# Attention 2 in 32-row quadrants, value products in 32 columns, and projections with the gate biases in their chunks

## The reference

```python
h = tok(x)                                   # layernorm, 768 -> 192, layernorm, class token: 197 x 192
# attention 1
q, k, v = split(layernorm(h) @ w_qkv.T)      # 12 heads of 64
q = q * rsqrt(norm(q over the heads) + 1e-8) # k likewise
h = h + softmax(q @ k.T / scale[head]) @ v @ w_out.T + b_out
# attention 2
x2 = layernorm(h)
probs = softmax(x2 @ Wg.T + bg); combine = the two largest of 8, the rest 0
hw = (x2 @ A + ba) * combine                 # 8 experts, rank 16: 128 columns
qkv = x2 @ Wqkv.T + bqkv + 2 * (hw @ Bm + combine @ bb)
q, k, v = split(qkv)                         # 12 heads of 16
h = h + softmax(q @ k.T / 4) @ v @ Wproj.T + bproj
```

## Time and profile before

| | |
|---|---|
| median of 3 runs | 4209.02 us (4180.69 to 4213.12) |
| the profiled execution | 4172.1 us, span 4170.0 us |
| TensorE busy | 3646.2 us, 87% |
| VectorE busy | 2701.7 us, 65% |
| ScalarE busy | 2236.3 us, 54% |
| GpSimd busy | 523.2 us, 13% |
| mean granted TensorE clock | 0.974 |

### The profile page before, as it was taken

How to read it: one execution, slowest core, us unless ns; L and a number is a source line. 1 busy time by engine, 2 the same in 40 slices (tenths; PEclk the granted TensorE clock), 3 DMA queues, 4 the chain that set the end, 5 groups by cost and what they waited for, 6 DMA issues and landing times.

```text
span 4170.0 us, 92080 instructions
## 1 busy us (share of the span) xinstructions
PE 3646.2 (87%) x37528; PEld 3010.9 (72%) x37528; DVE 2701.7 (65%) x6870; ACT 2236.3 (54%) x4033; POOL 523.2 (13%) x858
## 2 busy tenths in 40 slices
PE   3888988988988988889889889889889889898887
PEld 2777777777777777777777777777777777777776
DVE  4566666666676676676666666666766766766654
ACT  1555555555555555555555555555555555555553
POOL 1111101111101101111111111111011011011110
PEclk8999999999999999999999999999999999999997
DMA  3000000000000000000000000000000000000000
GB/s 84 9 9 16 16 9 16 16 9 16 16 9 16 16 9 16 16 9 16 9 15 16 9 16 16 9 16 16 9 16 16 9 16 16 9 16 16 9 4 4
DMA packets 26635, 60.62 MB, mean 15 GB/s; under 512 B 3626, under 2 KB 16557, under 8 KB 26222
## 3 DMA queue, kind: packets, MB, share of 16 engines
q1 hardware_dynamic: 26222, 54.73, 4.3%
HBM read 45.04 MB, written 9.68 MB: 13 GB/s over the span
## 4 chain that ended last, share of the span: by engine, by line
PE 59%; DVE 34%; ACT 3%; issue 2%; POOL 1%; DMA 0%; SPq 0%; DVEq 0%; ACTq 0%
PE psum L604 13%; DVE mx L952 13%; PE psum L638 6%; PE psum L610 6%; PE psum L577 6%; PE psum L668 3%; PE psum L543 3%; PE psum L533 3%; DVE kb L1047 3%; PE psum L661 3%; PE psum L640 2%; DVE qk_sq L925 2%; DVE qk L940 2%; PE psum L641 2%; PE psum L620 2%
## 5 line engine op out<-in xcount | busy, mean ns | idle before, releaser
L952 DVE TENSOR_REDUCE mx<-psum 99x4 f32<-99x788 f32 x768 | 703.6, 969 | 17.4 <-PE psum L561 10.4
L757 ACT ACTIVATE ebuf<-psum 99x788 f32<-99x788 f32 x768 | 604.9, 824 | 172.8 <-PE psum L593 160.6
L449 POOL TENSOR_TENSOR veps<-mv,eps_ln 99x2 f32<-99x2 f32 x256 | 49.7, 194 | 3005.9 <-DVE mv L861 2407.9
L638 PE MATMUL psum<-hn_s,qkv_w 96*128 96x197 f16 x2304 | 342.2, 254 | 44.2 <-ACT ss L730 43.0
L533 PE MATMUL psum<-hn_s,qk_w 128*128 128x197 f16 x3840 | 363.4, 250 | 1.2 <-DVE hn_s L918 1.2
L973 DVE TENSOR_TENSOR qk<-psum,rinv 128x197 f32<-128x197 f32 x384 | 137.5, 358 | 342.2 <-ACT rinv L766 342.2
L717 ACT ACTIVATE qk_sq<-psum 128x788 f32<-128x788 f32 x192 | 158.8, 827 | 352.5 <-PE psum L533 352.5
L533 PEld LDWEIGHTS psum<-hn_s,qk_w 128*128 128x128 f16 x3840 | 335.3, 98 | 7.5 <-DVE hn_s L918 1.5
L604 PE MATMUL psum<-ebuf,vx 98*64 98x197 f32 (+1 forms) x3072 | 332.7, 337 | 0.0
L591 PE MATMUL psum<-qa,ka 128*99 128x197 f16 x1536 | 289.2, 252 | 43.7 <-DVE qb L964 28.2
L604 PE MATMUL psum<-ebuf,ones_col 98*64 98x197 f32 (+1 forms) x3072 | 323.3, 330 | 0.0
(11 more groups left out here) (171 smaller groups left out, 7963.4 us busy)
## 6 DMA issues: line engine op xcount, KB each, us to landing
xb<-x_t SPq DMA_DIRECT2D x64, 591.0 KB, 3.7
out<-h SPq DMA_DIRECT2D x128, 73.5 KB
out<-h SPq DMA_DIRECT2D x64, 0.8 KB
vx<-w_qk SPq DMA_DIRECT2D x2, 384.0 KB
qk<-w_qkv SPq DMA_DIRECT2D x1, 720.0 KB
qk_sq<-w_emb SPq DMA_DIRECT2D x1, 576.0 KB
out_w<-w_out SPq DMA_DIRECT2D x1, 576.0 KB
vx<-w_qk SPq DMA_DIRECT2D x1, 576.0 KB
```

Source lines behind the costliest of these rows:

```text
L638: nc.tensor.matmul(o, qkv2_w[:, w, c, f], hn2_s[s][:, v, c, 0:NT], start=(c + w + v == 0), stop=False)
L757: nc.scalar.activation(ebuf[n % EBUFS][:].rearrange("p e a t -> p e (a t)"), psum[0:TR, b:b + 2, 0:2 * NT], ACT.Exp).then_inc(done, 1)
L952: nc.vector.tensor_reduce(mx[s][:, :, 2 * i:2 * i + 2].rearrange("p a e -> p e a"), psum[0:TR, b:b + 2, 0:2 * NT].rearrange("p e (a t) -> ...
```

## The change

**Attention 2 in quadrants.** Each head of 16 gets rows 32j to 32j+31 of the array. Three column blocks become two (`QKV2` from 960 to 704 columns). Two of the three groups of four heads share a block, and for them the keys are scaled with a mask that keeps one of two 16-row halves (`kmask`); the third has its own block. SM2 has three parts instead of six, each of 8 matmuls of 32 rows in four banks; ST2 has three parts of 32 matmuls in four banks: high x high, high x low, low x high and the negated maximum (`sel2`, `neg_t2`) for four heads. The eight masked copies are gone. The first two banks of SM2 and ST2 are released on their own (`rd_lo`). NT2 has one copy on ScalarE and none on VectorE.

**Value products in 32 columns.** PV has three parts of four heads instead of six of two: sums first, in a bank of their own, then the values in two halves of 32 columns. ScalarE starts on the sums (`sums_made`) before the values are done, and one multiplication of 394 columns replaces two of 197.

**Projections.** The hidden vector stands in a chunk of 128 rows and one of 64, which is there twice, once high and once low (`BIASED`). The last rows of the second take the gates (27 rows), so the bias product goes. A block takes eight matmuls. T2 makes 128 rows a chunk, and ScalarE doubles 64 columns of the layernorm's result first (`hn2_doubled`).

**Order and loads.** `ORDER` is new; one line of the old and one of the new stand in the diff. The weights need 49 load instructions on SyncE instead of 24, since they are placed piece by piece.

```diff
 ORDER = """
...
-N.2 -V2@2 -SM2.0@4 -SM2.1@2 N.3 -SM2.2@0 V.0@4 -SM2.3@2 -SM2.4@0 -SM2.5@6 V.1@4 SM.0@0 -NT2@7
+N.2 -V2@2 -SM2.0@4 -SM2.1@0 N.3 V.0@4 -SM2.2@0 V.1@6 SM.0@4 -NT2@0 SM.1@6 SM.2@2 -ST2.0@4 SM.3@0
...
-WIDE = ("QK", "V", "SM", "ST", "QK2", "SM2", "ST2")
+WIDE = ("QK", "V", "SM", "ST", "PV")
+QUAD = ("SM2", "ST2")
...
+            BIASED = ((0, 0, 0), (0, 1, 0), (1, 0, 0), (2, 0, 1), (3, 1, 1))
...
                     elif kind == "SM2":
-                        wait(pe, now, rd_sig["QK2"], ("QK2", s, 1))
-                        wait(pe, now, ka2_ready, ("QK2", s, 1))
-                        for e in range(2):
-                            h = 2 * i + e
-                            for t in range(2):
-                                mm = nc.tensor.matmul(ps(p, slice(0, TR), slice(NT * t, NT * t + NT), e),
-                                                      qa[s][:, h // 4, tile_cols(t)],
-                                                      ka[s][:, h, 0:NT], start=True, stop=True)
+                        wait(pe, now, high_QK2, ("QK2", s, 1))
+                        for t in range(2):
+                            for j in range(4):
+                                r = slice(32 * j, 32 * j + 32)
+                                mm = nc.tensor.matmul(ps(p, slice(0, TR), slice(NT * t, NT * t + NT), j),
+                                                      qh2[r, i // 2, tile_cols(t)], kh2[r, i, 0:NT],
+                                                      start=True, stop=True)
...
                     elif kind == "ST2":
+                        wait(pe, now, rd_sig["QK2"], ("QK2", s, 1))
                         wait(pe, now, rd_sig["NT2"], ("NT2", s, 0))
...
+                        for t in range(2):
+                            terms = ((kh2[:, i, tile_cols(t)], qh2[:, i // 2, 0:NT]),
+                                     (kh2[:, i, tile_cols(t)], ql2[:, i // 2, 0:NT]),
+                                     (kl2[:, i, tile_cols(t)], qh2[:, i // 2, 0:NT]),
+                                     (sel2[:, i, :], neg_t2[s][:, 0:NT]))
+                            for n, (left, right) in enumerate(terms):
+                                for j in range(4):
+                                    r = slice(32 * j, 32 * j + 32)
+                                    mm = nc.tensor.matmul(ps(p, slice(0, TR), slice(NT * t, NT * t + NT), j),
+                                                          left[r], right[r], start=(n == 0), stop=(n == 3))
                     elif kind == "PV":
-                        wait(pe, now, rd_sig["ST"], ("ST", s, i))
+                        wait(pe, now, rd_sig["ST"], ("ST", s, 2 * i + 1))
...
-                        for at in (0, NT):
+                        for c in (2, 0, 1):
                             for t in range(2):
                                 n = key_rows(t)
...
+                                    mm = nc.tensor.matmul(
+                                        ps(p, slice(32 * j, 32 * j + 32), slice(NT * (c % 2), NT * (c % 2) + NT), c // 2),
+                                        left, eb[0:n, j % 2, t, :], start=(t == 0), stop=(t == 1))
+                            if c == 2:
+                                mm.then_inc(sums_made[1], 1)
...
                     elif kind == "QK2":
                         wait(pe, now, rd_sig["T3"], ("T3", s, 0))
...
+                        for m in range(2):
+                            o = ps(p, slice(0, 128), slice(NT * m, NT * m + NT))
+                            f = slice(128 * (2 * i + m), 128 * (2 * i + m) + 128)
+                            for n, (w, v, c) in enumerate(BIASED):
+                                nc.tensor.matmul(o, qkv2_w[:, w, f], hn2_s[s][:, v, c, 0:NT],
+                                                 start=(n == 0), stop=False)
+                            for n, (w, v) in enumerate(SPLIT):
+                                mm = nc.tensor.matmul(o, lorab_w[:, w, f], hw_s[s][:, v, 0:NT],
+                                                      start=False, stop=(n == 2))
...
-                        if i == 1:
-
-                            wait(act, now, high_QK2, p)
-                            for j in range(4):
-                                a = nc.scalar.mul(ka[s][:].rearrange("p (g j) t -> p g j t", j=4)[:, :, j, :],
-                                                  high2[:], masks[:, j:j + 1])
-                            a.then_inc(ka2_ready[1], 1)
...
+                            for u in range(2):
+                                nc.scalar.mul(kh2[:, u, 0:NT], psum[:, b, 0:NT], kmask[:, u:u + 1])
+                            nc.scalar.mul(kh2[:, 2, 0:NT], psum[:, b, NT:2 * NT], 1 / WS).then_inc(high_QK2[1], 1)
...
-                            for j in range(4):
-                                a = nc.vector.tensor_scalar(
-                                    kb[s][0:64].rearrange("p (g j) t -> p g j t", j=4)[:, :, j, :], low2[:],
-                                    masks[0:64, j:j + 1], None, ALU.mult)
+                            for u in range(G2):
+                                a = nc.vector.scalar_tensor_tensor(
+                                    out=kl2[:, u, 0:NT], in0=pair[:, u // 2],
+                                    scalar=kmask[:, u:u + 1] if u < 2 else 1 / WS,
+                                    in1=kh2[:, u, 0:NT], op0=ALU.mult, op1=ALU.subtract)
```

## The result

The changed kernel takes 4264.33 us (median of four runs, 4261.64 to 4265.76) beside 4209.94 of the kernel before on the same chip: a ratio of 1.0133, 95% interval 1.0084 to 1.0182. It is slower by 1.3%, where I forecast 4155 us and a gain.

What follows compares the result with a forecast made beforehand. No engine alone sets the time: VectorE ends stage A and limits stage B, TensorE mainly stage C. Terms -2.5 + 3.4 - 2.1 and 0.4 for the clock make -0.8 us a half pass, -55 in all: 4155 us, range 4040 to 4300.

Steps and rivals of the forecast that it cites:

- stage A: From output projection OP to SM2.0's first maximum on VectorE, 30.4 us: gains 2.5 us a half pass (bounds 1.9 and 2.9).
- stage B: From SM2.0's first maximum to attention 1's negated maxima, 12.8 us: loses 3.4 us a half pass (bounds 1.4 and 4.8).
- stage C: From attention 1's negated maxima to the next OP, 19.8 us, mainly TensorE: gains 2.1 us (bounds 1.2 and 3.0).
- these 4.7 us: TensorE work saved in stage A: 3.8 us in QK2 and some 0.9 in V2, mostly hidden because VectorE ends the stage.
- the walk: Row-by-row timing of stage C: ST.0 at +1.1 us, PV.2 at +13.1, next OP at +17.7, a gain of 2.1.
- rival of two pairs: Groups of four in ST2 take 0.17 instead of 0.085 us: 1.4 us more in stage B, 4241 us; chance 0.10.
- The 0.9 us ahead of PV.2: Stage C: PV.2 stands right behind ST.5 and waits 0.9 to 1.0 us for its exponential on ScalarE.
- M2.0's place in VectorE's way: Stage B: PV2.0 and M2.0 ahead of SM.5 put negated maxima at 16.2 instead of 12.8 us; VectorE idles before M2.0.
- rival of a shorter chain: Chain to M2.0 in stage B is shorter, 2 of the 3.4 us don't show: 4028 us; chance 0.16.
- TensorE bounds everything: TensorE's ten microseconds of saved work a half pass come off whole: ratio 0.85, 3580 us; chance 0.05.
- The clock: TensorE nearly idle from V2's end to V.0: one fall to half clock every half pass, 0.4 us over today's mean.
- The clock stays down: Falls also land on thin TensorE stretches from V.1 to ST.0: 2.2 us a half pass over the sum, 4292 us; chance 0.27.

Runs made afterwards that it cites:

- run 9: Kernel before with the change's projections alone, plus extra unread matmuls ahead of T2, QK2.0 and SM2.0: 4106.82 us, ratio 0.9802.
- run 7: Changed kernel with its waits filled by extra matmuls, but the old value products of attention 1 (six parts of two heads): 4130.20 us.
- run 4: Changed kernel with SM.5 ahead of PV2.0 and NT right behind it, waits filled by extra matmuls: 3991.21 us, ratio 0.9559.
- run 2: Changed kernel with extra unread matmuls only in the waits of stage B and stage C, 80 a half pass: 4175.59 us, ratio 1.000.
- run 1: Changed kernel with 206 extra unread matmuls a half pass in TensorE's waits: 4082.73 us, 0.9778 of the kernel before.
- run 10: Changed kernel with extra unread matmuls only in stage A's waits, 126 a half pass: 4266.70 us, ratio 1.0185.
- run 11: Changed kernel, unfilled, reordered: SM.5 ahead of ST2.1, NT and ST.0 ahead of ST2.2, ST.4 and ST.5 ahead of PV.1: 4049.99 us, ratio 0.9667.
- run 13: Changed kernel, waits unfilled, with ten extra matmuls (0.49 us) on the path at the end of OP: 4263.43 us.
- run 14: Changed kernel with its waits filled by extra matmuls, plus ten more on the path at the end of OP: 4116.71 us.

## Why the prediction was wrong

**At full clock it was right, step by step.** The filled kernels, with the fall of the clock taken out of both sides, give each step apart (us a half pass):

| | forecast | measured, filled |
|---|---|---|
| stage A | -2.5 | 30.37 to 27.90, -2.5 |
| stage B | +3.4 | 12.82 to 16.09, +3.3 |
| stage C | -2.1 | 19.84 to 17.90, -1.9 |
| sum | -1.2 | 63.03 to 61.90, -1.1 |
| of it the projections (run 9) | | -0.7 |
| of it the value products (run 7) | | -0.8 |
| of it the rest, by subtraction: quadrants and order | | +0.4 |

"Little of these 4.7 us reaches the end, because VectorE ends the stage" holds: in the changed kernel QK2 takes 0.69 us a block (forecast 0.68), and the first maximum starts 6.87 us after N.0 (forecast 6.9). In stage C the terms of the forecast don't add up to its gain: 3.7 us of work less, against 2.4 to 2.5 us of new waits, leave 1.2 to 1.3. The 2.1 comes from the walk, and the measured 1.9 bears out the walk. A group of four takes 0.09 us. Timeline of the changed kernel, TensorE, the first and the last of ST2.0's eight groups:

```profile
2041.80 0.29 PE L615 MATMUL psum<-qh,kh 32*99 32x197 f16 x4 [0.95 <-DVE mx L1004]
...
2042.41 0.28 PE L615 MATMUL psum<-neg_t,sel 32*99 32x197 f16 x4
```

Seven steps in 0.61 us, 0.087 each, so the rival of two pairs is out. There my estimate from the Trainium skill (TensorE: Matmul & The Clock Gate, Part 3: Packing small matmuls), 0.11 us, was too high; the trace decides. The 0.9 us ahead of PV.2 are 0.97. M2.0's place in VectorE's way is real: run 4 takes 2.4 us from B by it, so the rival of a shorter chain is out too. "TensorE bounds everything" is far off. The first OP starts at 123.97 instead of 122.21, 2 us later (forecast 5), but in other runs with the same loads it starts between 122.34 and 124.38, so the start's cost isn't clear of its scatter. The end gives 8 us (forecast 10).

**The step that failed is the one headed "The clock":** "I expect a fall in every half pass, 0.4 us over today's mean." It is 2.95 falls, and they cost 64.85 - 61.90 = 2.95 us; the kernel before loses 63.21 - 63.03 = 0.2 in the profiled execution. The forecast looked for the falls in one place, ahead of V.0, and there it was about right: the short fall at 29.6 us costs nothing, the long one at 26 us 0.5 us (and 1.15 in run 2, where it comes at 28). It put three other places at nothing. The trace of the changed kernel has 62 half passes, and their stages price the falls against the filled kernel (us):

| | half passes | A | B | C |
|---|---|---|---|---|
| filled, no fall (run 1) | | 27.90 | 16.09 | 17.90 |
| falls at 26 (long), 40 and 47 us | 37 | 27.90 | 17.71 | 19.33 |
| falls at 9, 30 and 47 us | 22 | 29.23 | 16.10 | 19.36 |

So a fall after T2 (9 us) costs 1.3 us, the one from ST2.1 to PV2.0 (40 us) 1.1 of the 1.6 in B, and the one from ST.0 to PV2.1 (47 us) 1.4 to 1.5, in nearly every half pass. Of 0.93 to 0.96, the granted clock came to 0.898, and the forecast's own mark for being wrong was 0.9.

**The rival "The clock stays down" was the right mechanism.** It named the thin stretches of B and C and the steps in them (ST2.0, ST2.1, PV2.0, ST.0, PV2.1), and priced them at 2.2 us over my sum of -0.8; measured is +1.6, 2.4 over it, and its 4292 us are 0.7% over the measured 4264. What it missed is the fall in A, at T2's wait of 1.8 us. That wait was there before too, and only 2 of the 33 falls in 62 half passes of the profiled execution stood there, so the stretch itself isn't enough to tell. Those two half passes took 64.86 and 65.07 us instead of 63.01: the dear fall was in the trace of the kernel before, 1.5 to 1.9 us in stage A, while the forecast priced a fall by one of the cheap ones. I gave this rival 0.27 and should have given it most: its condition, "from the second such unit on", was met by my own walk, which had three such stretches.

**The size isn't a sum of falls.** Runs 10, 11 and 13 show that. Without filling, a half pass of 62.4 us at full clock (run 14) and one of 61.90 (run 1) both take 64.85, and one of 60.48 and one of 59.09 both take about 61.45. In these kernels the mean length settles on a value, and half a microsecond more or less of work inside changes only where the falls land. It isn't so in every kernel with falls: in run 2 every half pass has one or two falls, and they take between 62.3 and 64.6 us, 63.34 in the mean, which is neither of the two values. So what is mended isn't what is gained: run 10 filled with 126 of the 206 matmuls and gained nothing, run 2 with the other 80 and gained half. Why some kernels settle, and why at these lengths, isn't shown by these runs.

## What to carry to other kernels

Before TensorE's work is taken away where another engine ends the stage, ask what its clock will do in the gap. Here TensorE was idle for half or more of several stretches of a half pass, and the clock fell on the short steps behind them, ST2.1, PV2.0, ST.0 and PV2.1, which are on the path. Price a fall in each such place by itself: in this kernel one fall cost between 0 and 1.9 us, by where it stood. Try the changed kernel once with its waits filled by matmuls that nobody reads: that splits a result into design and clock in one run, and here it turned +1.3% into -2.2%. Judge variants of a loop filled against filled; unfilled, two orders that were 1.4 us apart measured the same, and a delay on the path cost nothing.

## What was unexpected of the hardware

- A kernel got 182 us faster by 206 more matmuls a half pass (run 1), and stayed equal with ten more on its path (run 13).
- Without an idle stretch of 2 us on TensorE (the longest two in the changed kernel's half pass above are 1.85 and 1.83 us) the clock still fell three times in 65 us. The Trainium skill (TensorE: Matmul & The Clock Gate, A second HAM failure mode: psum-queue depth-cycling) says that small idles between groups of matmuls are enough to make the clock swing; the trace agrees, with 0.83 to 1.68 us busy of 3.4 ahead of the four falls shown.
- A fall can last: 17 us at 0.50 in run 10, with TensorE busy for 13.84 of them.
- The kernel before itself varies with its falls: medians of 4175, 4190, 4209 and 4231 us beside the four groups of experiments, and the granted clock goes from 0.974 in a run of 4171 us to 0.956 in one of 4239. With its three waits filled its runs lie between 4155 and 4159.
